# Routing batch 0 earlier inside the attention steps, and another order of the shared experts' products

## What is computed

```python
x = x + tanh(g_xattn[0]) * attention(layernorm(x), ctx, pos)   # 32 heads of 8, softmax, @ Wout + bout
# mixture of experts on layernorm(x), 1024 rows:
shared = sum(relu(flat @ sw1[e] + sb1[e]) @ sw2[e] + sb2[e] for e in range(2)) / 2
probs = softmax(flat @ router_w + router_b)                    # 32 routed experts
topk_p, topk_i = top_k(probs, 6)
gates[row, topk_i] = topk_p / sum(topk_p)
routed = sum(gates[:, e] * (relu(flat @ rw1[e] + rb1[e]) @ rw2[e] + rb2[e]) for e in range(32))
x = x + tanh(g_ffn[0]) * (shared + routed)
```

## Time and profile before

| | us |
|---|---|
| median of 3 runs | 386.02 |
| lowest and highest run | 383.51, 388.6 |
| the profiled execution, its own time | 387.09 |
| its span, from the first to the last instruction | 385.3 |
| PE busy | 333.4 |
| DVE busy | 240.6 |
| POOL busy | 221.7 |
| ACT busy | 214.6 |

### The profile page before, as it was taken

The page is one execution under the profiler, slowest core; times in us unless marked ns, Lnnn a source line. Parts: engine busy times, 40 slices in busy tenths (PEclk is TensorE's granted clock), DMA queues, the critical chain, the costliest instruction groups (busy, mean ns, idle before and its releaser), DMA issues.

```text
span 385.3 us, 8620 instructions
## 1 busy us (share of the span) xinstructions
PE 333.4 (87%) x2574; PEld 262.3 (68%) x2574; DVE 240.6 (62%) x753; ACT 214.6 (56%) x537; POOL 221.7 (58%) x267
## 2 busy tenths in 40 slices
PE   8889999999899988786772999999999999999800
PEld 5567766666666664564541898999999999999700
DVE  7997788789789888569310355555555545445426
ACT  4795899979878877232130455555555555555400
POOL 8466332103013456757774288888788888787830
PEclk9999999999999999699786899999999999999965
DMA  7799999996004014613233488888888888897688
GB/s 227 208 309 310 308 326 315 320 237 205 4 2 134 19 60 125 204 60 117 101 116 125 128 125 144 137 151 138 139 146 147 142 143 141 138 146 108 76 195 282
DMA packets 63295, 62.20 MB, mean 161 GB/s; under 512 B 6258, under 2 KB 61588, under 8 KB 63252
## 3 DMA queue, kind: packets, MB, share of 16 engines
q1 hardware_dynamic: 48532, 44.60, 40.5%
q0 software_dynamic: 13680, 17.05, 27.4%
q10 hardware_dynamic: 1040, 0.01, 0.2%
HBM read 29.01 MB, written 32.63 MB: 160 GB/s over the span
## 4 chain that ended last, share of the span: by engine, by line
PE 55%; DVE 12%; issue 10%; POOL 9%; DMA 8%; ACT 5%; SPq 0%; POOLq 0%; DVEq 0%
PE psum L1608 14%; PE psum L1590 10%; POOL rows_by_block L502 7%; PE psum L1301 6%; PE psum L1348 5%; DVE nmax L906 5%; DMA sum<-ob,xs 5%; PE psum L1581 4%; PE psum L1599 3%; ACT probs L625 2%; PE psum L1319 2%; PE psum L1196 2%; PE psum L1282 2%; PE psum L1401 2%; POOL sum L546 2%
## 5 line engine op out<-in xcount | busy, mean ns | idle before, releaser
L546 POOL DMA_INDIRECT sum<-ob,xs x79 | 122.4, 1549 | 40.1 <-DVE ob L1166 26.9
L906 DVE TENSOR_REDUCE nmax<-psum 128x2 f32<-128x512 f32 x128 | 80.9, 683 | 13.2 <-PE psum L1301 12.3
L1608 PE MATMUL psum<-w,hT 88*128 (+1 forms) x316 | 81.5, 380 | 0.0
L625 ACT ACTIVATE probs<-psum 128x512 f32<-128x512 f32 x128 | 69.5, 599 | 15.3 <-PE psum L1319 13.8
L1166 DVE TENSOR_SCALAR ob<-psum,gate 128x256 f32<-128x256 f32 x79 | 38.2, 484 | 53.5 <-PE psum L1608 38.1
L755 ACT ACTIVATE hT<-psum,b1b 88x128 f32<-88x128 f32 x158 | 48.8, 357 | 35.6 <-PE psum L1599 34.6
L1590 PE MATMUL psum<-w,xT 128*128 x316 | 61.6, 318 | 0.3 <-ACT xT L746 0.3
L1608 PEld LDWEIGHTS psum<-w,hT 88*128 88x128 f32 (+1 forms) x316 | 53.8, 190 | 4.6 <-issue 0.3
L746 ACT ACTIVATE xT<-psum 128x256 f32<-128x256 f32 x79 | 30.3, 384 | 46.3 <-PE psum L1581 46.2
L502 POOL DMA_INDIRECT rows_by_block<-Vx,slot x48 | 47.6, 991 | 14.4 <-issue 14.1
L425 POOL CAST Qx<-nmax 128x8 fp32r<-128x8 f32 x32 | 6.3, 197 | 74.2 <-DVE nmax L906 74.1
(11 more groups left out here) (194 smaller groups left out, 468.6 us busy)
## 6 DMA issues: line engine op xcount, KB each, us to landing
rows_by_block<-blank SPq DMA_DIRECT2D x1, 10744.0 KB, 38.2
xs<-rows_by_block SPq DMA_DIRECT2D x79, 136.0 KB, 2.9
w<-in_L_ffn_rw_dram SPq DMA_DIRECT2D x2, 2816.0 KB, 22.1
w<-in_L_ffn_rw_dram SPq DMA_DIRECT2D x16, 352.0 KB
sum<-blank SPq DMA_DIRECT2D x3, 1152.0 KB, 13.4
w<-sum SPq DMA_DIRECT2D x12, 256.0 KB, 5.3
sum<-ob,xs POOLq DMA_INDIRECT x79
x_sb<-in_x_dram SPq DMA_DIRECT2D x4, 256.0 KB, 3.9
```

The source lines that it names most:

```text
L546: pool.indirect_dma_start(yd[i], bass.IndirectOffsetOnAxis(ap=xs[b % ROWS_AHEAD][:, X_ID:X_ID + 1].bitcast(U32), axis=0), ob[i][:, :], Non ...
L625: act.activation(probs[g % 2][:, :, n, :], st_bank(g, n)[:, :].rearrange("p (t q) -> p t q", t=TB), ACT.Exp, scale=SCALE).then_inc(exp_ok, 1)
L906: dve.tensor_reduce(nmax[i % 2][:, :, n], S_BANK[(4 * i + n) % SB][:, :].rearrange("p (t k) -> p t k", t=TB), AX.X, ALU.max, negate=True). ...
L1608: ins = pe.matmul(Y_BANK[b % 2][:, 0:D], hT[b % 2][0:rows, c, :], w2[0:rows, bass.ds(expert[b], 1), c, :].rearrange("p a n -> p (a n)"), s ...
```

## The change

Three things change, and no instruction is added or taken away.

1. Tables. Batch 0's routing moves: rows transposed in step 18 instead of 19, router scores in 19 instead of 20, counts in 22 instead of 24, and what follows them on ACT, DVE and POOL moves by as much. Batch 1's projections move later by one step, to 23 and 24 instead of 22 and 23. The normalised rows of batches 0 and 1 are written behind the second and fourth row maximum of steps 17 and 26 (before: behind the first and third of steps 18 and 26). POOL's `scales` for batch 1 come in step 25 instead of 24.
2. Dealing. Batch 0's transfers start in step 26 instead of 28. Eleven are issued in the steps instead of seven.
3. The tail on PE. Each `shared_out` moves back behind later pieces of work. The product for the blocks' experts and that for their biases stand apart now.

```diff
-        PROJ_STEPS = {NG * (b + 1) + 6 + t: (b, t) for b in range(B - 1) for t in range(TB)}
+        PROJ_AT = [14, 23, 30]
+        PROJ_STEPS = {PROJ_AT[b] + t: (b, t) for b in range(B - 1) for t in range(TB)}
-        ROWS_STEPS = {NG * b + 19: b for b in range(EARLY)}
-        SCORE_STEPS = {NG * b + 20: b for b in range(EARLY)}
-        COUNT_STEPS = {24: 0}
+        NORM_AT = [17, 26]
+        ROWS_STEPS = {NORM_AT[b] + 1: b for b in range(EARLY)}
+        SCORE_STEPS = {NORM_AT[b] + 2: b for b in range(EARLY)}
+        COUNT_STEPS = {NORM_AT[0] + 5: 0}
...
-            DEALT_AT = {28: (0, 2), 29: (2, 3), 30: (3, 5), 31: (5, 7)}
+            DEALT_AT = {26: (0, 2), 27: (2, 4), 28: (4, 6), 29: (6, 7), 30: (7, 9), 31: (9, 11)}
...
-                    if g == NG * b + 16:
+                    if g == NORM_AT[b] - 1:
                         scales(b)
...
-                if g == 25:
+                if g == NORM_AT[0] + 6:
                     blocks_needed(0)
-                if g == 26:
+                if g == NORM_AT[0] + 7:
                     places_early(0)
...
-                    at = i - NG * b
-                    if (at, part) == (18, 0):
+                    at = i - NORM_AT[b]
+                    if (at, part) == (0, 1):
                         dve.wait_ge(nstep_ok, b + 1)
                         dve.wait_ge(pv_mm, NG)
                         normalised_row(TB * b)
-                    if (at, part) == (18, 2):
+                    if (at, part) == (0, 3):
                         normalised_row(TB * b + 1)
...
             shared_transposed(0)
             counts(B - 2)
-            shared_out(0)
             shared_hidden(2)
             second_rows_transposed(B - 1)
             shared_transposed(1)
+            shared_out(0)
             router_scores(B - 1)
-            shared_out(1)
             shared_hidden(3)
             shared_transposed(2)
+            shared_out(1)
             counts(B - 1)
-            shared_out(2)
             shared_hidden(4)
             shared_transposed(3)
-            shared_out(3)
+            shared_out(2)
```

More of the change, by code:

```diff
@@ L680, in _ @@
                 step(i)
-                if i in (NG * b + 22 for b in range(EARLY)):
-                    gate_exponentials((i - 22) // NG)
+                if i - 4 in NORM_AT:
+                    gate_exponentials(NORM_AT.index(i - 4))
             exponentials(GROUPS - 3, 2)
@@ L998, in early @@
                         normalised_row(TB * b)
-                    if (at, part) == (18, 2):
+                    if (at, part) == (0, 3):
                         normalised_row(TB * b + 1)
-                    if (at, part) == (21, 0):
+                    if (at, part) == (3, 0):
                         scores(b)
-                    if (at, part) == (21, 1):
+                    if (at, part) == (3, 1):
                         then(eight_best(b))
-                    if (at, part) == (21, 2):
+                    if (at, part) == (3, 2):
                         where_best(b).then_inc(at8_ok, 1)
-                    if (at, part) == (22, 1):
+                    if (at, part) == (4, 1):
                         dve.wait_ge(exp_row_ok, b + 1)
@@ L1010, in early @@
                         then(choice_of(b))
-                    if (at, part) == (23, 0):
+                    if (at, part) == (5, 0):
                         mask_of(b)
-                    if (at, part) == (23, 2):
+                    if (at, part) == (5, 2):
                         gate_sums(b)
-                if (i, part) == (26, 1):
+                if (i, part) == (NORM_AT[0] + 7, 1):
                     dve.wait_ge(had_ok, 1)
                     block_ends(0, blocks[:, 0, :]).then_inc(upto_ok, 1)
-                if (i, part) == (27, 3):
+                if (i, part) == (NORM_AT[0] + 8, 3):
                     dve.wait_ge(placed_ok, 1)
@@ L1396, in output_projection @@
                 if b < B - 1:
-                    pe.wait_ge(t_ok, min(NG * (b + 1) + 6 + t + AHEAD + 1, GROUPS))
+                    pe.wait_ge(t_ok, min(PROJ_AT[b] + t + AHEAD + 1, GROUPS))
                     if t:
@@ L1407, in second_rows_transposed @@
                 if b < EARLY:
-                    pe.wait_ge(t_ok, min(NG * b + 19 + AHEAD + 1, GROUPS))
+                    pe.wait_ge(t_ok, min(NORM_AT[b] + 1 + AHEAD + 1, GROUPS))
                 if b == EARLY:
@@ L1419, in router_scores @@
                 if b < EARLY:
-                    pe.wait_ge(t_ok, min(NG * b + 20 + AHEAD + 1, GROUPS))
+                    pe.wait_ge(t_ok, min(NORM_AT[b] + 2 + AHEAD + 1, GROUPS))
                 for t in range(TB):
@@ L1432, in counts @@
                 if b == 0:
-                    pe.wait_ge(t_ok, 24 + AHEAD + 1)
+                    pe.wait_ge(t_ok, NORM_AT[0] + 5 + AHEAD + 1)
                 if b == 1:
@@ L1547, in _ @@
             shared_transposed(1)
+            shared_out(0)
             router_scores(B - 1)
-            shared_out(1)
             shared_hidden(3)
             shared_transposed(2)
+            shared_out(1)
             counts(B - 1)
-            shared_out(2)
             shared_hidden(4)
             shared_transposed(3)
-            shared_out(3)
+            shared_out(2)
             shared_hidden(5)
             shared_transposed(4)
+            shared_out(3)
             pe.wait_ge(later_ok, 1)
             pe.matmul(C_BE, every[:, :], later[:, :], start=True, stop=True).then_inc(be_mm, 1)
+            shared_hidden(6)
+            shared_transposed(5)
             pe.wait_ge(isbe_ok, 1)
@@ L1564, in _ @@
             ins.then_inc(b1_mm, 1)
-            for n in range(4, NT):
-                shared_out(n)
-                if n + 2 < NT:
-                    shared_hidden(n + 2)
-                if n + 1 < NT:
-                    shared_transposed(n + 1)
+            shared_out(4)
+            shared_hidden(7)
+            shared_transposed(6)
+            shared_out(5)
+            shared_transposed(7)
+            shared_out(6)
+            shared_out(7)
+            assert NT == 8
             expert = {}
```

2 lines of the change are left out of this document (1 added, 1 removed).

## The result

The changed kernel took 391.39 us in the median of 4 runs (390.01 to 393.59), the kernel before 386.58 in the same comparison (383.51 to 388.6, 4 runs). The ratio is 1.0151, 95% interval 1.0107 to 1.0194: slower by 1.5%. That is within the 2% that the forecast gave a chance of 0.93, but 4.0 us above its 387.4 and above its range of 384.0 to 390.0. The profiled execution of after took 393.59 us with a span of 391.8 (before 387.09 and 385.3), so the profile explains a loss of 6.5 us, of which the medians show 4.8.

What follows compares the result with a forecast made beforehand. It took POOL's thirty contiguous transfers behind batch 3's root, started by DVE's `veps`, as the bound. 0 + 0 + 0.3 + 1.3 - about 0.2 = +1.4 us on 386.02 gave 387.4, range 384.0 to 390.0.

Steps and rivals of the forecast that it cites:

- one for one: Attention steps: whatever they lose or gain was to pass in full into the tail and the kernel's end.
- signs of being wrong: Tail: root sooner than 168.4 plus the steps' shift, thirty transfers not contiguous, or blocks started on the last shared sum.
- Four transfers fewer: POOL behind the steps: four fewer transfers only lengthen its wait for `veps` from 2.53 to over 5 us; worth 0.
- Transfers in steps 26 to 31: POOL in the steps: six transfers in 26 to 28, four more in 29 to 31; 0, bounds 0 to 0.6 us.
- Moved pieces: PE in the steps: the shifted pieces of extra work keep the same sum, no step has two; 0.
- the untied knot: Steps 23 to 24: batch 0's mask and gate sums leave batch 1's residual step; gain 0.25, at most 0.42 us.
- The wait for `rstd`: DVE in steps 17 and 26: waits of 0.4 and 0.9 us before a normalised row, costing 0.3 and 1.3 us.
- the scan: Behind step 26: the scan moves out, a gain of perhaps 0.1 us; about 0.2 with rounding in the sum.
- The tail order: PE's tail: each `shared_out` one piece later, all under 6.2 us of slack; worth 0.
- the slow clock: Rival in PE's tail: the new pause brings the 1.2 GHz level through the shared work; 392.9 us, chance 0.05.

Runs made afterwards that it cites:

- e3: The kernel before with eleven instead of seven transfers dealt in steps 28 to 31, nothing else; 388.28 us against 387.15, ratio 1.0022.
- e1: The changed kernel's step tables and conditions with the dealing table and PE tail order of the kernel before; 394.83 us against 387.15, ratio 1.021.
- f6: The kernel before with batch 0's rows, scores, marks and gates a step earlier, batch 1 as before; 387.03 us against 386.68, ratio 1.0004.
- f5: The changed kernel with PE's transposes of steps 23, 26 and 27 put ahead of the third score product and done twice; 391.97 us against 386.68, ratio 1.0116.
- e2: The kernel before with only the change's order of the shared experts' products in PE's tail; 386.4 us against 387.15, ratio 1.0007.
- e4: The changed kernel with the normalised rows of batches 0 and 1 written a step later, in steps 18 and 27; 388.92 us against 387.15, ratio 1.0049.
- g1: f8 with nine instead of seven transfers dealt in steps 28 to 31 and one moved ahead of batch 3's root; 385.07 us against 385.95, ratio 0.9954.
- f8: The kernel before with eight idle identity products on PE ahead of batch 2's transposed rows; 385.2 us against 386.68, ratio 0.9967.
- g4: The changed kernel with e4's edit, two transfers moved ahead of batch 3's root, and 8 and 48 idle products in PE's pauses; 383.43 us against 385.95, ratio 0.9947.
- g2: f8 with 32 more idle products on PE ahead of the blocks; 383.56 us against 385.95, ratio 0.9966.
- g3: f8 with the change's tail order, nine transfers dealt in steps, one ahead of batch 3's root, 50 more idle products; 383.73 us against 385.95, ratio 0.9959.

## Why the prediction was wrong, point by point

*What bounds the kernel.* Right. The root of batch 3 sets the thirty transfers, these run without a pause (36.81 us for 29, 1.27 each), and the blocks start 4.61 us behind the last one, as before with 4.72. What the steps lose arrives at the end, but not "one for one", as the forecast had it (see below). One of its signs of being wrong did show: the root starts at 177.74, 1.6 us sooner than 168.44 plus the steps' shift of 10.89.

*Four transfers fewer: worth 0.* Right. POOL is idle 3.55 us ahead of the root, and 3.19 us more ahead of batch 1's first transfer; together 6.7 us, forecast more than 5 in one piece. e3 has the same by itself, and no gain.

*Transfers in steps 26 to 31: 0.* Right for the change's table, as far as the runs show it: e1, which deals as before did, is no faster than after. The forecast read that table wrong, though, with "four more in steps 29 to 31": steps 28 to 31 deal seven transfers in both kernels, and the four new ones are in 26 and 27. With eleven in steps 28 to 31, e3 loses one us in step 30.

*Moved pieces and the untied knot: -0.25.* Inconclusive. Where the clock stays up, step 23 takes 4.20 (e1) against 4.45, but steps 21 to 25 of e1 together take 19.52 us against 19.14 before. The knot moved to step 22, where DVE has the mask and the gate sums, and PE waits 0.53 us for a bank in after.

*The wait for `rstd`: 0.4 and 0.9 us, cost 0.3 and 1.3.* The waits were 0.43 and 1.02. The cost of the first is 0.95 us (steps 17 to 20, 15.83 against 14.88), and f6 has 0.8 for its steps as a whole. For the second f5 has 4.21 against 3.46 at full clock, 0.75, with its own doubled transposes in it. With 0.38 in steps 21 to 25 (e1) the steps at full clock cost about 2.1 us in all, forecast 1.4 with bounds of -0.8 and 3.4. The mechanism and the range were right. (The sum takes off "about 0.2" for the scan and rounding where the text has "perhaps 0.1" for the scan; no run shows either.)

*The tail order: 0.* Right, by e2. The pause ahead of batch 3's rows is 2.35 us, forecast about 2.

*The step that failed* is the one behind the sum: the terms were priced at PE's full clock, and the slow clock was a rival "in the tail" alone, with a chance of 0.05, "if the clock then fell and stayed down to the end of the shared work". It fell in the steps. The first fall costs 5.83 - 4.20 = 1.6 us in step 23. The second costs steps 27 to 29 18.20 - 12.21 = 6.0 us, and step 26 another 0.8 (4.99 against f5's 4.21). That is 8.4 of the 10.5 us that steps 3 to 32 lost, and it makes the second wait, of 1 us, cost 7.5 (6.8 and its own 0.75). With it, and with 4.0 us off for what came back (next point), the sum gives 386.0 + 1.4 + 8.4 - 4.0 = 391.8; that is an account made afterwards from one pair of profiled executions, not a check. The rows that would have warned were in use, 0.62 and 0.50 behind pauses in the tail; I applied them to the pause that the change opens there and not to the ones that it opens in the steps.

*What came back.* `values` of step 32 starts 10.89 us late (159.49 against 148.60): 0.43 of that was there at step 3, and 10.46 come from the steps. The root is 9.30 late. The tail's slow stretch, 0.50 at 158 to 162 us before, is shorter after (0.64 at 168 to 172), and the work up to the root takes 1.6 us less. That is not the change's doing: from the last `values` to the root it takes 15.2 us before and 13.7 after, but 13.6 in e2, whose code up to there is before's, and 15.3 in f5, whose code is after's. The transfers gave 0.24 back, the way from the last of them to the first result 0.6, the blocks from the first result to the last 1.1 (148.54 against 149.62), and the rest came at the end. In all 4.4 came back, and 0.4 + 10.5 - 4.4 = 6.5 is left between the profiled executions. The medians differ by 4.8, since the profiled execution was the slowest of its four and the one with the lowest clock.

*How far the cause is shown.* That the loss is in the tables is shown (e1, e2, e3). The second fall is in both traces that have the pauses of 0.23 and 0.59 us behind the wait for `rstd` (after, e1), with the same periods to the hundredth in steps 26 to 28. It is gone when the rows no longer stand right behind `veps` (e4), and with the wait left in and PE kept busy (f5), in one trace each; e4's timed runs bear it out, f5's do not. That moving batch 0's rows, scores and gates is harmless by itself is shown within 0.4% (f6). That the pauses cause the falls is then the best reading, not a proof: each test moved other instructions too. For the second fall the reading is strong. The first, 1.6 us, is less surely the change's: in e1 and f5 it comes at another place, behind the wait for `lg` that before has too, and g1 shows a fall there with before's steps. In after and e4 it comes about 2 us behind a pause of 0.53 us in step 22, which before does not have; e1 has that pause and no fall behind it. What in the tables makes this pause no run tested by itself. Open is also what ended the long stretch at 148.6 us.

## What to carry to other kernels

On an engine whose clock is granted, a wait has two prices: its own length, and what the clock does behind it. Here DVE's wait of 1 us cost 6.8 us of clock in both traces that have it as changed, while PE's own wait of 0.84 us in the steps cost none in before and a fall in g1. So look for the stretches in which the granted clock is 1.00 and PE has little idle time, and count every new pause there as a chance of losing the clock, not as a certain loss. Work is worth moving ahead only on the engine that is late: POOL was 2.53 us early, and giving it less to do made it 6.7 us early. A few idle products in a pause that can't be closed are cheap to try: the medians came out 0.9 to 2.5 us lower here (f8, g1 to g4), though the intervals of f8, g2 and g3 reach 1.0.

## What the hardware showed that was not expected

The clock fell after pauses of 0.23 and 0.59 us, in a stretch where PE was busy for 3.20 of 4 us. It then stayed at 0.50 while PE's rows were busy 9.99 of 10 us. The Trainium skill, page "TensorE: Matmul & The Clock Gate", section "Part 1: The HAM clock gate", has activity release the throttle; the trace doesn't contradict it, since the clock did return at about 148.6 us with PE still at work, but the first fall was over at 118 us, after at most 4, and the second lasted some 17, so that sentence alone gives no price here.

Two executions of the same steps, with PE busy for the same 6.05 us in 7 us, differed in whether the clock fell (0.68 in g1 and 1.00 in f8 behind it). The same pause of 0.84 us had a fall behind it in 3 traces of 13. One profiled execution is one draw; the clocks of the timed runs are the better witness.

Eight products of a 128x128 fp32 identity (2.05 us, 0.256 each) put into a pause of 2.05 us left the clock at 1.00 behind it in f8, where before it went to 0.50.
